# Router products two per step and one unit each, with routing and two residual additions moved later, in a one-core decoder kernel

## The reference

```python
x = x + cross_attention(layernorm(x), ctx)                 # 32 heads, 64 context rows per batch
x = x + ffn(layernorm(x), int4 gate/up/down weights)       # inner size 1792
x = x + recurrent(ctx, layernorm(x), ...)                  # 256 steps, one after the other
x = x + experts(layernorm(x), ...)                         # 16 experts of 56, best 2 per row
# recurrent, one step for the 4 batches:
e = va . tanh(enc_proj + s @ Wa_s.T + conv(alpha) @ Wa_f.T + ba)
alpha = softmax(e); g = alpha @ ctx
y = tanh(g @ L_gy.T + b + s @ L_sy.T) @ L_yy.T + b
s, c = lstm(tgt @ L_ys.T + s @ L_ss.T + g @ L_gs.T + b, c)
# experts, the part that the change is about:
logits = h @ gate_w.T          # the router: 512 -> 16
probs = softmax(logits); vals, idx = top_k(probs, 2); vals /= sum(vals)
```

## Time and profile before

| | us |
|---|---|
| median of 3 runs | 1504.61 |
| lowest, highest | 1502.2, 1511.74 |
| the profiled execution: its time | 1507.64 |
| the profiled execution: its span | 1505.8 |

### The profile page before, as it was taken

One profiled execution on the slowest core, in us unless ns is written; L12 is line 12 of the kernel. 1 busy time (PEld: TensorE's weight loads), 2 busy tenths in 40 slices (PEclk: granted clock), 3 DMA queues, 4 the chain that ended last, 5 costly groups with the idle time before them and its releaser, 6 DMA issues.

```text
span 1505.8 us, 43803 instructions
## 1 busy us (share of the span) xinstructions
PE 1384.3 (92%) x17408; PEld 911.5 (61%) x17408; DVE 909.9 (60%) x4453; ACT 586.7 (39%) x2367; POOL 211.5 (14%) x704
## 2 busy tenths in 40 slices
PE   3566887999999999999999999999999999999988
PEld 1345665566665676766666665566665665666556
DVE  3664754366655666665666667666655666566643
ACT  3563662234333344333344434443333333333321
POOL 1001102011111111111111112221100011101111
PEclk8666897999999999999999999999989999899989
DMA  8462220000000000000000001200000000000000
GB/s 280 187 221 78 72 76 4 1 3 2 2 2 2 2 2 2 2 2 2 2 2 3 2 25 51 60 23 2 2 16 2 2 2 9 9 3 2 9 9 15
DMA packets 23874, 44.94 MB, mean 30 GB/s; under 512 B 8788, under 2 KB 12035, under 8 KB 23668
## 3 DMA queue, kind: packets, MB, share of 16 engines
q1 hardware_dynamic: 23668, 42.14, 8.6%
HBM read 40.04 MB, written 2.10 MB: 28 GB/s over the span
## 4 chain that ended last, share of the span: by engine, by line
PE 83%; DVE 7%; ACT 5%; issue 4%; SPq 1%; DMA 1%; POOL 0%; DVEq 0%; ACTq 0%; POOLq 0%
PE bank L1940 9%; PE bank L1861 9%; PE bank L1654 9%; PE bank L1883 8%; PE bank L1671 6%; PE bank L1915 6%; PE bank L1692 4%; PE bank L1889 4%; PE bank L1637 3%; PE bank L1897 3%; PE bank L1924 3%; PE bank L1903 2%; PE bank L1631 2%; PE bank L1539 2%; ACT interT L1217 2%
## 5 line engine op out<-in xcount | busy, mean ns | idle before, releaser
L1861 PE MATMUL bank<-ctx_lgs,identb 128*128 128x512 f16 (+2 forms) x685 | 191.8, 357 | 0.0
L1940 PE MATMUL bank<-ker_mem,uh 128*128 128x128 f32 x1020 | 184.0, 304 | 1.4 <-DVE ker_mem L1140 1.1
L1940 PEld LDWEIGHTS bank<-ker_mem,uh 128*128 128x128 f32 x1020 | 136.8, 194 | 67.4 <-DVE ker_mem L1140 50.1
L1654 PE MATMUL bank<-xT,wbig 128*128 128x256 f16 x1008 | 161.9, 274 | 0.0
L1459 ACT ACTIVATE xs<-gat 64x8 f32<-64x8 f32 x255 | 52.9, 207 | 245.6 <-DVE gat L1136 245.5
L1445 ACT ACTIVATE ker_mem<-bank 128x128 f16<-128x128 f32 x256 | 71.1, 278 | 185.5 <-PE bank L1883 185.5
L1450 ACT ACTIVATE eh<-bank,nmx 128x8 f16<-128x8 f32 x256 | 68.5, 268 | 173.6 <-PE bank L1906 173.6
L1671 PE MATMUL bank<-wbig,interT 128*128 128x512 f16 x378 | 124.3, 395 | 0.0
L1140 DVE TENSOR_TENSOR ker_mem<-inv,ahn 128x128 f32<-128x128 f32 x510 | 124.2, 285 | 0.0
L709 POOL TENSOR_TENSOR sscale<-ex,rinv 128x8 f32<-128x8 f32 x256 | 51.6, 201 | 505.5 <-DVE rinv L1125 505.5
L705 POOL COPY sscale<-s 64x4 f32<-64x4 f32 x256 | 59.5, 232 | 389.1 <-DVE s L1155 389.1
(11 more groups left out here) (234 smaller groups left out, 3191.2 us busy)
## 6 DMA issues: line engine op xcount, KB each, us to landing
kbd<-d_keys SPq DMA_DIRECT2D x32, 256.0 KB, 3.9
wbig<-d_gate_qT SPq DMA_DIRECT2D x4, 896.0 KB, 9.9
wbig<-d_up_qT SPq DMA_DIRECT2D x4, 896.0 KB, 20.7
wbig<-d_down_qT SPq DMA_DIRECT2D x1, 3584.0 KB, 13.2
sscale<-d_down_sT SPq DMA_DIRECT2D x4, 768.0 KB, 9.3
x_sb<-d_x SPq DMA_DIRECT2D x16, 128.0 KB, 3.0
d_out<-x_sb SPq DMA_DIRECT2D x16, 128.0 KB, 2.4
sscale<-d_gate_sT SPq DMA_DIRECT2D x2, 896.0 KB, 8.3
```

The source lines that it names most:

```text
L1654: last = mm(tile_bank(n)[:, lo:lo + QC], w[wi][:, kt, it * P:(it + 1) * P], x_part[q % 2][xi][:, kt, :], start=(kt == 0 and wi + xi == 0), ...
L1861: mm(bank[7][:, 0:n], identb[:], hg2[:, 0].rearrange("p h g -> p (h g)")[:, 0:n], start=True, stop=True)
L1940: mm(bank[0][:, 0:P], uh[:, h, :], qv[:, h, :, :], start=False, stop=False, skip_group_check=True)
```

## The change

- `expert_routing` on PE yields a UNIT behind each router product, where it did so behind every second one. For quarters 0 and 2 two products are due per step, where it was four; quarter 1 keeps four.
- Quarter 0: the router starts one step earlier (89 instead of 90), and routing, exp, top, turned, high and weights come one step later.
- Quarter 2: the router starts at the same step (219), routing, exp and top come two steps later, as do turned, high and weights, and `E[2]` goes from 227 to 229: all of quarter 2's expert work comes two steps later.
- `GATES[2]` goes from (101, 108) to (102, 109): layernorm, transposes and products of the recurrence input of quarter 2's rows come one step later, on DVE, POOL, PE and ACT.
- The additions of the feed-forward sums of quarters 1 and 2 (`hidden_added`) come one step later: steps 39, 46, 90 and 97.

No operation is added or taken away in the real work; what changes with the charges is how many `keep_busy` products are issued, and in which slot each real product stands.

```diff
--- before.py
+++ after.py
@@ -341,7 +341,7 @@
 
         SPLIT = 134
         LAST_ADDED = (136, 143)
-        E = (158, 195, 227)
+        E = (158, 195, 229)
 
         def expert_step(q, it):
 
@@ -352,14 +352,14 @@
             return expert_step(q, IT1) + 4 * p
 
         LN2 = (None, None, 2, 55)
-        GATES = (None, (38, 45), (101, 108), (155, 165))
+        GATES = (None, (38, 45), (102, 109), (155, 165))
         Y = (68, 128, 196, S)
         PRELUDE = (dict(outputs=0, tanh=2, rows=(4, 6), added=(6, 8), moments=(9, 11), rstd=(11, 13), normal=(13, 15), turn=(16, 18),
-                        copy=(18, 20), low=(20, 22), router=22, routing=24, exp=24, top=25, turned=31, high=32, weights=33),
+                        copy=(18, 20), low=(20, 22), router=21, routing=25, exp=25, top=26, turned=32, high=33, weights=34),
                    dict(outputs=0, tanh=2, rows=(4, 6), added=(6, 10), moments=(12, 14), rstd=(16, 18), normal=(18, 20), turn=(21, 23),
                         copy=(23, 25), low=(25, 27), router=55, routing=57, exp=57, top=58, turned=65, high=66, weights=67),
                    dict(outputs=0, tanh=2, rows=(4, 10), added=(6, 12), moments=(15, 16), rstd=(17, 18), normal=(18, 19), turn=(20, 21),
-                        copy=(21, 22), low=(22, 24), router=23, routing=25, exp=25, top=26, turned=31, high=32, weights=32))
+                        copy=(21, 22), low=(22, 24), router=23, routing=27, exp=27, top=28, turned=33, high=34, weights=34))
 
         def pace(q):
 
@@ -957,7 +957,7 @@
                     for it in range(IT0):
                         yield from gate_tile(q, it)
                     if q < NQ - 1:
-                        yield from hidden_added(q, [down_step(q, p) + 7 for p in range(2)])
+                        yield from hidden_added(q, [down_step(q, p) + 8 for p in range(2)])
                 yield from merged(hidden_added(NQ - 1, LAST_ADDED), weight_pieces())
                 for q in range(NQ - 1):
                     for it in range(IT1):
@@ -1824,14 +1824,13 @@
             def expert_routing(q):
                 work = router(q)
                 for unit in range(8):
-                    yield from paced(prelude_step(q, 'router') + unit // 4)
+                    yield from paced(prelude_step(q, 'router') + unit // (4 if q == 1 else 2))
                     if unit == 0:
                         pe.wait_ge(s["xT_ready"], ln4(q, 1) + 1)
                         if q == 1:
                             pe.wait_ge(s["rin_ready"], 8)
                     next(work)
-                    if unit % 2 == 1:
-                        yield UNIT
+                    yield UNIT
                 work = turn_weights(q)
                 for unit in range(2):
                     yield from paced(prelude_step(q, 'turned'))
```

## The result

The changed kernel is slower: 1516.45 us against 1505.77 us, each the median of 22 runs, ratio 1.0052 with a 95% interval of 1.0038 to 1.0065 (here and below the ratio is an estimate over all runs; the quotient of the two medians is 1.0071). The forecast was 1501.5 us in a range of 1496 to 1508, so it had the wrong sign and missed the range. What happened is the mechanism of the second rival, more time at half clock near the thin places (the slots where router products stand in place of wide ones), but mostly in quarter 0, where the rival did not look, and at more than twice its price: it had +4.1 us.

The account below looks back on a forecast made before the run. The bound was a loop through PE, ACT and DVE with a floor of 4.44 or 4.50 us a step. Gains of 2.63 us at full clock plus 0.45 for a half-clock step made 3.1: median 1504.61 to 1501.5 us, range 1496 to 1508.

Parts of the forecast that it names:

- the second rival: Quarters 1 and 2: clock falls more, further half-clock steps at 2.23 us each; three give +4.1 us, 1508.7; chance 0.18.
- the slot prices at full clock: Router steps: 4.50 us with two products in slot 3, 4.95 with two each in slots 1 and 2, 4.50 with one each.
- 0.45 + 0.45: Step 184, wholly at half clock: router gain of 0.45 us doubled, so 0.45 more, called an estimate.
- the moved stall: ACT's wait moves from step 116 to 118 and shrinks, 0.80 to 0.56 us over the floor: 0.24 us gained.
- Steps 89 and 92 cost nothing more: Quarter 0's router spread over steps 89 to 92: the two added steps stay at 4.50 us, covered by ACT's exponentials.
- 2.63 us gain: Whole kernel at full clock: 0.54 + 0.90 + 0.78 + 0.24 + 0.17 us saved.
- cost at nothing: Work moved past other queues, such as quarter 0's expert choice on DVE and late statistics on POOL: priced at zero.
- the 0.11 us in hand: Slack between the end of an addition's second half, 694.97, and slot 1's start, 695.08, read as step 94.
- the clock term: Half-clock stretches around steps 183, 184 and 218 to 220 left as they were in the profiled execution.
- 90 and 91 stayed at 1.00: Quarter 0's router steps, losing only slot 3, kept full clock; cited for the rival where the clock falls less, chance 0.20.
- 0.90 + 0.45: Quarter 1's router, steps 183 and 184: 0.90 us gained at full clock, 0.45 more for half-clock step 184.
- 0.78 us: Quarter 2's router, steps 219 to 222: 18.78 us before, 18.00 after, with one product each in slots 1 and 2.

Follow-up runs that it names:

- copy_sooner: Changed kernel with ACT's copy of quarter 0's second slot due one step sooner, `copy=(18, 19)`; 1.0063 of the kernel before, median 1517.03 us.
- gates_only: Kernel before with only `GATES[2]` moved one step later, to (102, 109); 0.9985 of the kernel before.
- q0_one_later: Changed kernel with quarter 0's router in steps 90 to 93, routing, exp and top one step later too; 0.9988 of the kernel before, median 1506.76 us.
- after_shift_2: Changed kernel with two extra 512-column products that nobody reads in slot 1 of step 81; 1.0060 of the kernel before.
- before_shift_2: Kernel before with two extra 512-column products that nobody reads in slot 1 of step 81; 0.9978 of the kernel before.
- before_shift_5: Kernel before with five extra 512-column products that nobody reads in slot 1 of step 81; 1.0017 of the kernel before.
- q0_only: Kernel before with only quarter 0's part of the change, `GATES[2]` and the later additions; 1.0042 of the kernel before.
- after: The changed kernel itself, with the whole change, against the kernel before; 1516.45 us against 1505.77 us, ratio 1.0052.
- wide_shift_5: Changed kernel, ACT's copy one step sooner, half a unit per quarter 0 router product, five extra wide products in step 81; 1.0051 of the kernel before.
- wait_covered: Changed kernel with five unread 512-column products ahead of the wait for ACT's copy in step 89; 1.0042 of the kernel before.

## Why the prediction was wrong, point by point

**Right: the slot prices at full clock.** Two router products in slot 3 cost nothing: steps 89 and 90 of copy_sooner are 4.50. Two in each of slots 1 and 2, read as 4.95 from two rows, took 4.93 in gates_only, whose step 183 kept the full clock; one in each, with two in slot 3, took 4.49 in q0_one_later (windows, step 183 of each):

```profile
1120.80:1125.73 4.93, 4.90 (x72) 3.33 (x69) 2.51 (x16) 1.49 (x7) 0.38 (x2) 1.00 0.24 55
```

```profile
1121.53:1126.02 4.49, 4.46 (x70) 3.29 (x68) 2.50 (x16) 1.49 (x7) 0.38 (x2) 1.00 0.26 60
```

Step 184, wholly at 0.50 of the clock both times, went from 7.18 to 6.33 us: 0.85 less, where 0.45 + 0.45 was forecast. In quarter 2, one in each of slots 1 and 2: forecast 4.50, measured 4.50 in steps 219 to 221 of after_shift_2, whose clock stayed up there (windows, steps 218 to 221):

```profile
1287.82:1292.33 4.51, 4.51 (x66) 2.63 (x64) 2.49 (x15) 2.46 (x9) 1.05 (x3) 1.00 0.00 0
1292.33:1296.83 4.50, 4.45 (x68) 2.90 (x66) 3.13 (x17) 1.49 (x7) 1.05 (x3) 1.00 0.02 5
1296.83:1301.33 4.50, 4.47 (x68) 2.90 (x66) 2.50 (x16) 1.50 (x7) 1.05 (x3) 1.00 0.25 58
1301.33:1305.83 4.50, 4.47 (x68) 2.90 (x66) 2.48 (x15) 1.49 (x7) 1.05 (x3) 1.00 0.01 4
```

**Right: the moved stall.** Steps 116, 117, 118 of the changed kernel: forecast 4.50, 4.50, 5.06.

```profile
819.04:823.53 4.49, 4.42 (x71) 3.26 (x69) 2.80 (x16) 1.76 (x8) 1.05 (x3) 1.00 0.00 0
823.53:828.03 4.50, 4.38 (x71) 3.04 (x69) 2.84 (x17) 2.27 (x10) 0.38 (x2) 1.00 0.01 4
828.03:832.99 4.96, 4.45 (x73) 3.14 (x70) 2.80 (x16) 2.34 (x9) 1.05 (x3) 1.00 0.00 0
```

ACT's tanh in step 118 waited 1.21 us for PE. Step 120, forecast at 4.50, has that length in every profile with the moved `GATES[2]` in which its clock was full.

**Wrong: "Steps 89 and 92 cost nothing more".** The step followed every list but one to its last item: the router needs ACT's copies, two of them due at one place, and the second runs a place later than its number. The page of before had no wait there because step 90 comes after it. It is 0.98 us in step 89 at full clock, more than a third of the 2.63 us gain.

**Wrong: two of the terms "cost at nothing".** Step 94 of the changed kernel, in which DVE now begins the choice of experts, took 4.86 us at full clock against 4.50 before, and step 106, in which POOL works on the late statistics beside DVE's layernorm (L992, 0.96 us where it was 0.78), 4.71 against 4.51. Every profile with quarter 0's part has both where its clock was full. What holds step 94 was not followed. In one reading the text has the wrong step: the addition that ends at 694.97 stands at the end of step 89, not in step 94; the 0.11 us in hand is as read.

At full clock, taken from the profiles in which each step had it, the gains of the sum came to about 2.7 us and these three costs to 1.5, so the change was worth 1.2 us and not 2.63. The profiles account for the rest: 71.7 - 34.1 = 37.6 us more at half clock in the loop, at 0.26 each, is 9.8 us, less 1.2 is 8.6; the loop is 8.7 us longer.

**Wrong, and the larger part: the clock term.** The sum read which stretches were at half clock off one execution and left them as they are ("The forecast leaves these stretches as they are"). In quarter 0 that meant none; the changed kernel has 20.5 us there, worth about 5 us of the 6.7 that steps 89 to 96 lost. The sign was open from the start: the whole gain of 2.63 us at full clock equals 10 us at half clock by the line above, while the same instructions in steps 128 to 181 differ by 24 us of half clock from profile to profile. The rival named the mechanism and the break-even but gave it 0.18, looked for it in quarters 1 and 2, and priced three steps; quarter 0 decided, because "90 and 91 stayed at 1.00" was taken as a property of the kernel. gates_only shows that it was a property of that execution.

**Quarters 1 and 2.** The terms of 0.90 + 0.45 and 0.78 us are not seen in the whole: steps 182 to 188 took 35.20 before and 35.03 after, and over the twenty profiles 33.1 to 35.2 with four products a step for 2 units and 32.9 to 35.1 with a unit for each; steps 214 to 224 took 52.1 to 59.3 with no order between the two forms. They are seen at equal half clock. With 23.9 us of it, steps 214 to 224 took 57.59 to 57.60 us in before_shift_2, before_shift_5 and q0_only and 56.82 to 56.85 in after, q0_one_later and wide_shift_5: 0.76 less, forecast 0.78. With 10.2 us, steps 182 to 188 took 34.84 to 35.20 in five unchanged ones and 34.13 in the one changed, copy_sooner: 0.7 to 1.1 less. What the slots save there, a stretch of half clock gives or takes.

The rule of the Trainium skill that was weighed, in "TensorE: Matmul & The Clock Gate", section "What's actually happening", that activity releases the throttle, pointed to the right side. Its time was said to be the second rival's, 1508.7 us; measured were 1516.45. The share of time that PE is busy does not tell the places apart, though: in steps 91 and 92 of the changed kernel PE was busy for 6.12 of 6.12 and 6.54 of 6.54 us, and the clock was at 0.50.

**What stays open.** That the loss is time at half clock, set off by quarter 0's part (with the additions that go with it), is shown. That it is the lost wide columns behind step 89 which bring the clock down is supported and not settled: a wide product beside the routers lowered the ratio at each of the three places, by 0.9% (against copy_sooner), 0.7 and 0.2%, but place alone moves the wide kernel by 0.8%, and the wide product also brings the feed-forward sum forward, which was not tried apart. Why four thin steps from 90 on do less harm than from 89 on is not settled: step 89 stands one wide step behind the f32 transposes of steps 84 to 87, step 90 two; that was argued, not tried.

## What to carry to other kernels

Where a loop sits on the edge of the clock's fall, a fill may not be waste: look at what a rearrangement puts in place of wide products in each slot, and treat the granted clock of one profile as one draw. Compare the mean clock of all runs of both kernels, and profile the same kernel moved by a fraction of a microsecond, before a gain of less than 0.5% is believed. Compare slot prices at equal half clock: there the forecast's 0.78 us showed as 0.76, and in the whole not at all. When work is moved a step earlier, follow every producer to the place where its last item really runs, not to the number it is due at. A wide product beside narrow ones costs little (0.05 us a step here) and came with 0.9, 0.7 and 0.2% less time at three places.

## What the runs showed of the hardware that was not expected

- The clock fell with the wait gone: in wait_covered five products of 512 columns ran without a gap through the old wait, and half clock followed for 20.5 us.
- A microsecond at half clock cost 0.26 us here, in 20 profiles of the loop and over 376 executions.
- 0.36 us of extra work ahead did not make the kernel slower (0.9978, interval 0.9963 to 0.9993), and 1.00 us made it 0.4% slower than that: between two and five extra products of 0.21 us each the median moved by 7.0 us (1505.52 to 1512.53).
- The same 54 steps (128 to 181), with the same instructions, took 244.8 to 252.3 us, with 0 to 23.9 us of half clock.
